# Two-layer transformer block on one core: GpSimd's sum behind the rounding of the maxima, ScalarE's square two units later, the scan's step length laid in its PSUM bank, the experts' statistics spread over five pairs

## The reference, cut to what matters

```python
# layer 0, attention: 16 heads of 8, two score maps per head, causal
comb = softmax(s1) - lam * softmax(s2)
out  = comb @ v                                   # 16 values per head
normed = (out - mean(out)) * rsqrt(var(out) + 1e-5)
x = x + ga * ((normed * (1 - LAM_INIT)) @ Wo)
# layer 0, feed-forward of 512 hidden units with sin and relu
# layer 1, attention: a state space scan, 16 states n per feature d
u  = silu(conv3(h)); B, C = split(u @ W_bc + b_bc)
dt = softplus((u @ W_dt + b_dt) @ W_dtp + b_dtp)  # step length
state[t] = exp(A[d, n] * dt[t]) * state[t-1] + B[t, n] * h[t] * dt[t]
y[t] = sum_n C[t, n] * state[t]  + h[t] * D
# layer 1, feed-forward: 64 experts of 64 units, the best 8 of each token, and a shared expert
```

## Time and profile before

| | us |
|---|---|
| median of three runs | 1438.47 (1436.85 to 1441.33) |
| the profiled execution | 1435.74 |
| its span, first to last instruction | 1434.0 |
| attention, some | 0 to 660 |
| feed-forward | 660 to 780 |
| scan | 780 to 1040 |
| experts | 1040 to 1434 |

### The profile page before, as it was taken

One profiled execution on the slowest core, in us unless ns is written; L12 is line 12 of the kernel. 1 busy time (PEld: TensorE's weight loads), 2 busy tenths in 40 slices (PEclk: granted clock), 3 DMA queues, 4 the chain that ended last, 5 costly groups with the idle time before them and its releaser, 6 DMA issues. The chain is left out here.

```text
span 1434.0 us, 26470 instructions
## 1 busy us (share of the span) xinstructions
PE 1198.4 (84%) x8837; PEld 561.1 (39%) x8837; DVE 1126.1 (79%) x1923; ACT 1074.9 (75%) x1719; POOL 834.9 (58%) x812
## 2 busy tenths in 40 slices
PE   4489898989898989885875788776679999999998
PEld 3234343434343434332453223232234444444443
DVE  5678888888888888885976999999957776777653
ACT  2178878787878787774966889885467787778775
POOL 3034656565656565540001899899547777777776
PEclk8589999999999999997997899998889999999999
DMA  5341414141414141100004799888477768766884
GB/s 132 104 132 53 141 40 140 41 140 41 140 40 141 41 139 47 46 2 1 0 2 125 266 306 299 299 283 264 166 175 185 178 178 191 189 177 178 194 199 121
DMA packets 123690, 198.63 MB, mean 139 GB/s; under 512 B 24604, under 2 KB 60088, under 8 KB 123576
## 3 DMA queue, kind: packets, MB, share of 16 engines
q1 hardware_dynamic: 122136, 195.08, 47.8%
q10 hardware_dynamic: 1440, 2.10, 0.5%
HBM read 167.76 MB, written 28.84 MB: 137 GB/s over the span
## 5 line engine op out<-in xcount | busy, mean ns | idle before, releaser
L1071 DVE TENSOR_REDUCE bmax<-p1b 128x4 f32<-128x512 f32 x640 | 405.6, 685 | 82.6 <-PE p1b L777 78.0
L698 ACT ACTIVATE pT<-p2b 128x512 f32<-128x512 f32 x640 | 348.6, 598 | 92.0 <-PE p2b L830 90.3
L2220 POOL TENSOR_TENSOR hid_l<-e_hid,w_experts 128x1024 f16<-128x1024 f32 (+1 forms) x136 | 281.2, 2085 | 104.4 <-ACT w_experts L2355 103.5
L2454 DVE TENSOR_TENSOR e_hid<-ub,w_experts 128x1024 f32<-128x1024 f32 x128 | 155.8, 1223 | 121.4 <-ACT ub L2366 113.0
L648 POOL TENSOR_SCALAR_AFFINE_SELECT pT<-pT 128x512 f32<-128x512 f32 (+1 forms) x192 | 148.0, 787 | 164.4 <-ACT pT L698 164.4
L848 PE MATMUL ob<-pT,vs 128*32 128x384 f32 (+3 forms) x2048 | 187.4, 452 | 8.8 <-ACT o_sb L704 6.9
L1923 PE MATMUL yb<-ch,ident 128*128 128x512 f32 x256 | 135.1, 659 | 46.7 <-POOL ch L1893 46.5
L2355 ACT ACTIVATE w_experts<-e_hid 128x1024 f16<-128x1024 f32 (+1 forms) x136 | 139.4, 1025 | 38.0 <-DVE e_hid L2454 37.9
L2366 ACT ACTIVATE ub<-ub 128x1024 f32<-128x1024 f32 (+1 forms) x136 | 134.0, 985 | 37.9 <-PE ub L2271 36.1
L777 PE MATMUL p1b<-w_high 48*128 48x128 bf16 (+2 forms) x1792 | 130.0, 248 | 30.9 <-DVE bmax L1071 30.7
L830 PE MATMUL p2b<-w_high 50*128 50x512 bf16 (+3 forms) x1024 | 125.4, 302 | 2.7 <-ACT pT L698 2.1
(11 more groups left out here) (314 smaller groups left out, 2205.0 us busy)
## 6 DMA issues: line engine op xcount, KB each, us to landing
w_experts<-shares SPq DMA_DIRECT2D x256, 256.0 KB, 4.3
brow<-bc_rows SPq DMA_DIRECT2D x64, 512.0 KB, 4.0
crow<-bc_rows SPq DMA_DIRECT2D x64, 512.0 KB, 5.3
q_stacks<-w_low SPq DMA_DIRECT2D x96, 128.0 KB
k_stacks<-w_low SPq DMA_DIRECT2D x96, 128.0 KB
w_high<-q_stacks SPq DMA_DIRECT2D x128, 96.0 KB, 2.3
w_high<-k_stacks SPq DMA_DIRECT2D x128, 96.0 KB, 2.3
w_high<-nparts SPq DMA_DIRECT2D x128, 4.0 KB
```

The costliest lines, as they stand in the source:

```text
L698: act.activation(pT[:, g2 % 2, stored(u), :], p2b[bank_of(g2, u)][:, :], ACT.Exp, scale=SCALE).then_inc(exp_done, 1)
L1071: dve.tensor_reduce(to, bank, AX, ALU.max).then_inc(first_read, 1)
L2220: pool.tensor_tensor(flat(hid_l[:, rounded(p), 0:n, :]), flat(hid[:, place(p), 0:n, :]), rounded_half(p, 0, n), ALU.subtract).then_inc(spl ...
L2454: dve.tensor_tensor(h, u, flat(share[:, p % SHARES, :, :]), ALU.mult).then_inc(hid_ready, 1)
```

## The change

Six edits. In attention GpSimd's addition L634 moves behind the rounding of the maxima and the clearing of the last pair in its slot; ScalarE's square moves from unit 4 to unit 6; VectorE's sum of squares from unit 7 to unit 9, and the beginning of the root from unit 9 of slot 5 to unit 1 of slot 6. In the scan, ScalarE copies `dt` into the bank `dtxb` (`lay_step`), and VectorE multiplies there in place; `times_input` moves behind `run(7)` and the residual. The first of these copies stands at the end of ScalarE's step 8 of the feed-forward. In the experts the statistics are spread over pairs 11 to 15, and the loop over rounds 1 to 5 is written out.

```diff
-SQ_AT = 4
-RC_AT, SUM_AT, START_AT, MERGE_AT = (3, 9), (5, 7), (5, 9), (6, 6)
+SQ_AT = 6
+RC_AT, SUM_AT, START_AT, MERGE_AT = (3, 9), (5, 9), (6, 1), (6, 6)
...
-                if post and g == 5 and not alone:
-                    pool.wait_ge(pool_own, pb * 2 + 2)
-                    pool.tensor_tensor(og[:, :, :], og[:, :, :], o2[:, :, :], ALU.add).then_inc(og_ready, 1)
...
+                if post and g == 5 and not alone:
+                    pool.wait_ge(pool_own, pb * 2 + 2)
+                    pool.tensor_tensor(og[:, :, :], og[:, :, :], o2[:, :, :], ALU.add).then_inc(og_ready, 1)
...
+    def lay_step(self, act, b):
+        act.wait_ge(self.dt_ready, b + 1)
+        act.activation(self.dtxb[:, :], self.dt[:, b % 2, :], ACT.Copy).then_inc(self.dt_laid, 1)
+
     def times_input(self, dve, b):
-        dve.wait_ge(self.dt_ready, b + 1)
-        dve.tensor_tensor(self.dtxb[:, :], self.dt[:, b % 2, :], self.hT[:, b % 3, 1:S + 1], ALU.mult).then_inc(self.dtx_ready, 1)
+        dve.wait_ge(self.dt_laid, b + 1)
+        dve.tensor_tensor(self.dtxb[:, :], self.dtxb[:, :], self.hT[:, b % 3, 1:S + 1], ALU.mult).then_inc(self.dtx_ready, 1)
...
                     front.copy_bc(act, 1)
                     front.copy_z(act, 1)
+                    front.lay_step(act, 0)
...
+                if back:
+                    act.wait_ge(dBx_ready, (r + 1) * PAIRS + 2)
+                    front.lay_step(act, r + 1)
...
-                    if back and m == PAIRS - 2:
-                        dve.wait_ge(dBx_ready, (r + 1) * PAIRS + 2)
+                    if back and m == PAIRS - 1:
                         front.times_input(dve, r + 1)
...
-            with eng.Fori(1, B - 2) as r:
+            for r in range(1, B - 2):
                 step(r, pre=True, main=True, post=True, ahead=True)
...
-                def next_stats():
-                    entry.batch_stats(dve, b + 1)
+                def next_stats(p):
+                    if p == 11:
+                        entry.stat_sums(dve, b + 1)
+                    elif p == 12:
+                        entry.stat_start(dve, b + 1)
+                    elif p > 12:
+                        entry.stat_newton(dve, b + 1, p - 13)
...
-                        if ahead and p == 12:
-                            next_stats()
+                        if ahead and p < PAIRS:
+                            next_stats(p)
```

More of the change, by code:

```diff
@@ L1225, in __init__ @@
                                     "t1_ready", "z_psum", "zb_ready", "ee_ready", "dt_ready", "dtx_ready"))
-        self.size_ready, self.bc_saved = sem("s_size_ready"), sem("bc_saved")
+        self.size_ready, self.bc_saved, self.dt_laid = sem("s_size_ready"), sem("bc_saved"), sem("s_dt_laid")
         self.dve_stats, self.factors_ready, self.pool_log = sem("s_dve_stats"), sem("s_factors_ready"), sem("s_pool_log")
@@ L1707, in scale_shares, with stat_sums @@
         act.activation(self.turned_shares, bank[0:E, :], ACT.Copy, scale=W_SCALE).then_inc(self.shares_ready, 1)
-    def batch_stats(self, dve, b):
+    def stat_sums(self, dve, b):
         link = Chain(dve, self.dve_stats, b * STAT_LINKS).link
@@ L1714, in batch_stats, with stat_start @@
         link(last)
-        dve.sem_inc(self.passed, 1)
+    def stat_start(self, dve, b):
+        link = Chain(dve, self.dve_stats, b * STAT_LINKS + 1).link
         for c in range(TILES):
@@ L1719, in batch_stats, with stat_newton @@
         link(dve.tensor_scalar(self.var[:, :], self.stat[:, :, 1], EPS, None, ALU.add))
-        rsqrt_steps(dve, link, self.var[:, :], self.half[:, :], self.rstd[:, :], self.rtmp[:, :])
+        rsqrt_start(dve, link, self.var[:, :], self.half[:, :], self.rstd[:, :], self.rtmp[:, :])
+    def stat_newton(self, dve, b, n):
+        link = Chain(dve, self.dve_stats, b * STAT_LINKS + 6 + 3 * n).link
+        rsqrt_newton(dve, link, self.half[:, :], self.rstd[:, :], self.rtmp[:, :])
+    def batch_stats(self, dve, b):
+        self.stat_sums(dve, b)
+        self.stat_start(dve, b)
+        for n in range(3):
+            self.stat_newton(dve, b, n)
     def gates(self, dve):
```

## The result

The changed kernel takes 1426.8 us (median of 8 runs, 1422.3 to 1432.5) against 1437.5 us (8 runs, 1435.9 to 1441.3): the ratio is 0.9924, with a 95% interval of 0.9907 to 0.9941. It is faster; the forecast was 1421.4 us. Its runs spread over 10 us, those of before over 5.5. The profiled execution took 1424.91 us, with a span of 1423.2.

The account below looks back on a forecast made before the run. TensorE was taken to bound attention and experts, VectorE the scan. -5.5 + 3.4 - 4.5 - 10.5 = -17.1 us on the profiled 1435.74 gave 1418.6; with the median 2.7 above, 1421.4 us, range 1411 to 1434.

Parts of the forecast that it names:

- Attention, 5.5 predicted: Attention, seven rounds: 5.5 us gained, two thirds of rounds keeping the clock; bounds 8.4 us gained and 3 us lost.
- The two stands: Attention, start of slot 6: TensorE's one stand of 2.01 us becomes two, 1.3 and 1.5 us, with 1.4 us work between.
- the clock's part: Attention: if TensorE's clock stays up, 0.8 us more, 1.2 us a round; if it falls, between +0.5 and -0.4 us.
- End of the feed-forward, 3.4 lost: Feed-forward's end, once: multiplication and save come after ScalarE's copy behind its exponential, so the scan starts 3.4 us later.
- The scan, 4.5 gained: Scan, seven rounds: VectorE's multiplication reads PSUM, 0.66 us instead of 1.89; 4.5 us gained, bounds 0 and 7.4.
- ScalarE's chain hold rounds 1 to 5: Scan: ScalarE's work from `dA` on starts 1.2 us later, so these rounds gain only some 0.4 to 0.5 us.
- A quicker VectorE meets these rows sooner, so I take nothing for it: Scan: VectorE's waits for `brow`, 3.2 us before, were given no size in the forecast.
- The experts, 10.5 gained: Experts, six rounds: spread statistics shorten TensorE's stands, 1.9 us a round; 10.5 us gained, bounds 13.5 and nothing.
- `e_hid(15)` ends at 1236.55 instead of 1238.33: Experts, round's end: with Newton steps fitting between GpSimd's `hid_l`, VectorE finishes pair 15 earlier; one TensorE stand goes, another becomes 0.4 us.
- a second catch by GpSimd: Experts: two or more Newton steps caught each round, each further one costing 2.1 us; 1444.5 us, chance 0.06.
- a PSUM operand of the old price: Scan: the copy doesn't shorten VectorE, the bank's port costing the same; 0 for 4.5, 1426 us, chance 0.06.
- The first rival: Attention: the clock falls all the same and the second stand eats the gain; 1427 us, chance 0.14.

Follow-up runs that it names:

- e1: The kernel before with the change's attention edits alone: 1434.3 us, ratio 0.9977.
- e2: The kernel before with the change's scan edits alone (copy into the bank, multiplication behind it): 1438.8 us, ratio 1.0003.
- e6: The changed kernel with ScalarE's first copy of the step length moved ahead of its copies and exponential of batch 1: 1424.2 us, 0.9897 of before.
- e7: The changed kernel with both repairs, the save behind the load of pair 15 and the first copy sooner: 1418.5 us, 0.9862 of before.
- e11: The changed kernel, fetching only the first expert's (or pair's) part of each chunk of experts' weights loaded during the scan: 1423.5 us, 0.9892 of before.
- e4: The changed kernel with SyncE's save of the next batch's shares moved behind the load for pair 15: 1420.5 us, 0.9879 of before.
- e8: The kernel before with only attention's inverse root split, its four instructions standing one each ahead of four maxima: 1429.9 us, ratio 0.9935.
- e10: The change's scan and experts edits with both repairs, and attention's inverse root in four pieces instead of its attention edits: 1412.2 us, 0.9815 of before.

## Why the prediction held, and where it did not

The forecast of 1421.4 was 5.4 us below the median: too much for the experts (4.7 us) and for attention, a little too little for the scan. Its terms:

- **Attention, 5.5 predicted.** 3.3 us by e1 (interval 1.1 to 5.6), 5.1 us on average by the profiles: the six rounds from the first to the last `merged` take 426.3 to 427.1 us (mean 426.6) in six kernels with attention as before, 419.0 to 425.1 us (mean 421.5, from 424.1, 419.2, 425.1, 419.8, 419.0 and 422.0) in six with the change's edits. The two stands came where they were worked out (1.3 and 1.5 predicted, 1.38 and 1.15 measured), the clock's part too, in two sizes that were off: a round with the clock up gains 1.7 us and not 1.2 (the second stand is 0.35 us shorter than reckoned), but half of the rounds keep it and not two thirds: in these six profiles the clock fell behind 20 of 42 pairs of stands, in the other six behind all 42 of the long ones. So the gain is not 0.8 us in each round but 1.7 or about nothing. That two errors of opposite sign leave the average near 5.5 is luck. It is tempting to lay the wider spread of the changed kernel's runs (10 us against 5.5) to this, but e2, with attention as before, spreads over 10.8 us as well.
- **End of the feed-forward, 3.4 lost.** Right, step by step, and shown by undoing it in e6 and e7: from exponential to first dBx it is 1.32 us again. That these 3.5 us come back in the whole time is not shown (e6).
- **The scan, 4.5 gained.** 5.0 us in the changed kernel's profile, and e2 gives no net gain that can be measured where 4.5 less 3.4 would be 1.1, which its interval allows. The number came partly by luck: the prediction had ScalarE's chain hold rounds 1 to 5, and in the changed kernel's profile VectorE waits for `dA` once, 0.5 us, while rounds 2 and 3 lose their gain to waits for `brow`. The chain shows itself in e2, e6 and e11 (5.1, 6.3 and 7.0 us). The multiplication fell to 0.69 us as taken from the row with a PSUM operand. "A quicker VectorE meets these rows sooner, so I take nothing for it" was too kind: those waits grow from 3.2 to 4.4 us in the changed kernel, and in e2, where the waits for `brow` and `dA` are 8.0 us, the scan takes 271.8 us, 1.7 less than the 273.5 before. Over seven and six profiles the edit is worth 3.5 us (274.9 to 271.4). Which rounds lose changes from kernel to kernel.
- **The experts, 10.5 gained: the step that failed.** 5.8 us by the profile. Two sizes in it are wrong. Writing out the loop was taken at 0.1 us a round and is worth 0.7, most of it VectorE's pauses ahead of `e_hid`. And "`e_hid(15)` ends at 1236.55 instead of 1238.33" followed ScalarE, VectorE and GpSimd, but not SyncE's queue: with VectorE on time the load of the shares was late next, and `e_hid(15)` waited 0.98 us for it. The rest of the order was as written: each Newton step of the changed kernel waits for `hid_l` at most once, and none for 2 us. (The second stand was reckoned from 1.59 us, where the row has 1.43.) With the load repaired (e4) the stage gains 12.4 us, above the 10.5 and within the 13.5 given as bound.
- **Rivals.** Neither a second catch by GpSimd nor a PSUM operand of the old price came. The first rival (the clock falls anyway) came in half of the rounds. The lower end of the range is looser than its own sum: 8 + 6 + 12 less 3.4 from 1438.5 gives 1415.9, not 1414.

The single parts give 0.9977, 1.0003 and 0.9969, together 0.5% where the whole shows 0.76%; with intervals of 0.13 to 0.18% each, that difference is no finding. The Trainium skill ("SBUF — State Buffer", section "SBUF: two separate sides") has an exclusive lock between VectorE and GpSimd, held for a whole instruction; the traces agree, as each long instruction ends 0.02 to 0.03 us behind a `hid_l`. What did not come is the worst that the prediction drew from it, nine instructions that lose 2.1 us each: one instruction in each of two steps waited and took 1.27 and 1.02 us, and before them the one of `e_var`, 0.97.

## What to carry to other kernels

When a stand of the bounding engine is taken away, follow every queue whose work the late engine had hidden, the one that only issues transfers above all: here a wait in it held every load behind it. Look at what an edit rewrites in passing; here writing out a loop gave more (3.9 us) than the edit that it came with, until that edit's own obstacle was gone (then 7.3). And where a stage's length depends on whether the clock falls, count rounds of either kind in several profiles instead of averaging one.

## What the hardware showed that I had not expected

- In a loop with a run-time counter, an `e_hid` behind a chained instruction stood 0.19 to 0.22 us on VectorE, five times in each round; written out it stood 0.03 us, and a round of the experts was 0.73 us shorter (47.80 to 47.07).
- The same pair of stands left TensorE's clock at 2.4 GHz in some rounds and at 1.2 GHz in others of one execution (69.9 or 71.4 us a round). Of the shorter pairs of e8 and e10 (1.08 and 0.54 us) one in ten was followed by a fall; their three other falls came behind stands of 1.20, 1.55 and 1.56 us, and a stand of 1.22 us in e10 was followed by none. What decides between them is open.
